# Windowed attention on one core: where the softmax's reciprocal sums are applied, and by which engine

## The chip, the cores and the metric

One core of a Trainium2 chip runs one program. Its engines are named here as in the profile: TensorE (PE, with its weight loads as PEld), VectorE (DVE), ScalarE (ACT), GpSimd (POOL) and SyncE (SP). The metric is the device time of the whole program in microseconds (us). All data is float32 unless a row says otherwise.

## The reference, cut to what matters

The program is a chain of layers over x of 8 x 256 x 128. Two of them are six-layer transformers with windowed attention, and the change lies in these alone. One such layer, for each of the 8 batch rows of 256 positions, with 16 heads of 64:

```
q, k, v = split(x_shifted @ Wqkv)                # 128 -> 3 * 1024
q, k = rotary(l2norm(q)), rotary(l2norm(k))
# windows of 32: a query sees its own window and the one before, causal
sim  = einsum('bhwie,bhwje->bhwij', bq, bk2) * 8
attn = softmax(where(mask, -big, sim))
out  = einsum('bhwij,bhwje->bhwie', attn, bv2)
x    = x + out @ Wo
x    = x + feed_forward(shift(x))                # 128 -> 2 * 341 -> 128, gelu
```

Softmax divides each row of exponentials by its sum. The division may come before the product with V (on the probabilities) or after it (on the context).

## The kernel before, in words

A transformer runs as 48 **turns** (6 layers x 8 batch rows), and there are two transformers, so 96 turns. A turn T has 8 **slots** p; slot p belongs to one **pair** of heads. Each engine has one queue, written out by hand in `pe_window`, `act_window`, `dve_window` and in the loop for GpSimd, and each executes its queue in order; semaphores tie the queues together. Work of several turns is interleaved: in the slots of turn T the engines do the attention of T, the projections ("chunks") and rotations of T + 1, the output product of T - 1 and the feed-forward of T - 2 and T - 3.

The attention of one pair p goes through these steps, with the line of the profile in brackets:

- `pe_scores` (L1716) writes the scores of both heads into banks 0 and 1; VectorE's `dve_negmax` (L2090) adds the mask, writes the result into `c.pairs` and reduces it to a row's extreme; ScalarE's `act_probs` (L1983) takes the exponential in place in `c.pairs`, in four instructions, and gives the row sums.
- `dve_recip` (L2099) takes the reciprocal of the four sums of each partition. `pool_spread` (L1944) copies each reciprocal 64 times into `c.spread` (128 x 256).
- `pe_turn_probs` (L1728, L1729) transposes the unnormalised probabilities into bank 2 in four transposes, at the head of slot p. `act_copy_probs` (L1990) copies them out to `c.pairsT`; `dve_turn_prev` (L2110) transposes the small corner of the window before.
- `pe_shares` (L1738) transposes `c.spread` in two transposes into the upper half of bank 4 or 5, one slot later. `pe_weigh` (L1750) multiplies V with the turned probabilities into the lower half of that bank. ScalarE's `act_copy_shares` (L1995) copies the upper half out, and VectorE's `dve_share` (L2104) multiplies the lower half by it, which gives `ctxT`.

Of the other work, these steps stand in the same queues. TensorE's chunk products (L1784) of turn T + 1, two in each of slots 0 to 5, use banks 6 and 7 in turn. A q or k chunk is squared and copied by ScalarE (L2003, L2007: `act_copy_chunk`, in the next slot of its queue), summed and rotated by VectorE (L2121, L2129: `dve_rotate`), and only then is its bank free for the chunk after the next. A v chunk is copied by ScalarE alone (L2010). GpSimd's `pool_prepare` multiplies by the cosines (L1960), adds (L1967) and scales the keys (L1973): three instructions in slots 1 and 4, four in slots 2 and 5, two in slots 3 and 6, none in 0 and 7. The turned queries are copied by ScalarE (`act_copy_q`, L2015) and the turned keys by VectorE (`dve_copy_k`, L2115). VectorE's `dve_roots` (L2145 to L2151) is a chain of twelve small dependent instructions, in slots 2 and 6; in slot 2 the feed-forward's statistics (L2161 to L2166) stand before it. The output product of T - 1 (L1819) and half of the feed-forward (L1850) are TensorE's in slot 6.

The order inside slot p before: TensorE turns p, turns the shares of p - 1, makes the scores of p + 2, weighs p - 1, then the other work, then two chunks. ScalarE copies the chunks of slot p - 1, copies the turned p, takes the exponentials of p + 1 and copies the shares of p - 1. VectorE takes the reciprocal of p, applies the shares to p - 2, turns the corner of p, rotates, and reduces the scores of p + 2.

Of the kernel before, what the change touches and what calls it, by code (L numbers as in the profile page):

```python
# [16 lines left out]
P = 128  # L17
# [76 lines left out]
def allocate(nc, ctx):  # L94
# [37 lines left out]
    c.shares = sb("shares", [P, 2, S])  # L132
    c.recip = sb("recip", [P, 2, 32])
    c.spread = sb("spread", [P, 2, S])
# [1492 lines left out]
def windowed_transformers(nc, sem, c, name, io):  # L1627
# [7 lines left out]
             "probs_ready", "probsT_in_psum", "probsT_ready", "prev_ready", "recip_ready", "spread_ready", "ctx_in_psum", "shares_ready", "ctx_ready",  # L1635
# [8 lines left out]
     s.probs_ready, s.probsT_in_psum, s.probsT_ready, s.prev_ready, s.recip_ready, s.spread_ready, s.ctx_in_psum, s.shares_ready, s.ctx_ready,  # L1644
# [51 lines left out]
    def run(number):  # L1696
# [24 lines left out]
        def pe_turn_probs(pe, T, p):  # L1721
            pe.wait_ge(s.probs_ready, T * PAIRS + p + 1)
            if T * PAIRS + p > T0 * PAIRS:

                pe.wait_ge(s.probsT_ready, T * PAIRS + p)
            for side in range(2):
                probs, out = c.pairs[:, 2 * (p % 4) + side, :], c.bank[2][:, S * side:S * side + S]
                pe.transpose(out[:, 0:P], probs[:, 0:P], c.ident[:, :])  # L1728
                last = pe.transpose(out[:, P:2 * P], probs[:, P + WINDOW:2 * P + WINDOW], c.ident[:, :])  # L1729
            last.then_inc(s.probsT_in_psum, 1)  # L1730

        def pe_shares(pe, T, p):
            pe.wait_ge(s.spread_ready, T * PAIRS + p + 1)
            if T * PAIRS + p - 1 > T0 * PAIRS:

                pe.wait_ge(s.ctx_ready, T * PAIRS + p - 1)
            for t in range(HALVES):
                pe.transpose(c.bank[4 + p % 2][:, S + t * P:S + (t + 1) * P], c.spread[:, p % 2, t * P:(t + 1) * P],  # L1738
                             c.ident[:, :])

        def pe_weigh(pe, T, p):
            pe.wait_ge(s.probsT_ready, T * PAIRS + p + 1)
            pe.wait_ge(s.prev_ready, T * PAIRS + p + 1)
            if p == 0:
                pe.wait_ge(s.chunk_copied, (T + 1) * N_CHUNKS)
            out = c.bank[4 + p % 2]
            for kt, q0, q1 in ((0, 0, P + WINDOW), (1, P, S)):
                at = 0 if kt == 0 else P + WINDOW
                for side in range(2):
                    last = pe.matmul(out[DH * side:DH * side + DH, q0:q1], V[T % 2][:, kt, 2 * p + side, :],  # L1750
                                     c.pairsT[:, 2 * (p % 2) + side, at:at + q1 - q0], start=(kt == 0), stop=(kt == 1),
                                     skip_group_check=True)
            last.then_inc(s.ctx_in_psum, 1)
# [133 lines left out]
        def pe_window(pe, T):  # L1887
            following = has_turn(T + 1)
            for p in range(PAIRS):
                pe_turn_probs(pe, T, p)  # L1890
                if p >= 1:
                    pe_shares(pe, T, p - 1)
                elif has_turn(T - 1):
                    pe_shares(pe, T - 1, PAIRS - 1)
# [24 lines left out]
                if p == 5 and has_turn(T - 2):  # L1919
                    pe_turn_normed(pe, T - 2)  # L1920

        def pe_tail(pe):
            L = T1 - 1
            pe_shares(pe, L, PAIRS - 1)
# [115 lines left out]
        def act_window(a, T):  # L2040
            following = has_turn(T + 1)
            for p in range(PAIRS):
                if following:
                    for i in ACT_CHUNK_SLOTS.get(p, ()):
                        act_copy_chunk(a, T + 1, i)
                    if p == 6:
                        act_copy_q(a, T + 1, 0)
                act_copy_probs(a, T, p)
# [13 lines left out]
                if p >= 1:  # L2062
                    act_copy_shares(a, T, p - 1)
                elif has_turn(T - 1):
                    act_copy_shares(a, T - 1, PAIRS - 1)
# [6 lines left out]
        def act_tail(a):  # L2072
            L = T1 - 1
            act_copy_shares(a, L, PAIRS - 1)
# [27 lines left out]
        def dve_share(v, T, p):  # L2102
            v.wait_ge(s.shares_ready, T * PAIRS + p + 1)
            v.tensor_tensor(ctxT[T % 2][:, p, :], c.bank[4 + p % 2][:, 0:S], c.shares[:, p % 2, :],  # L2104
                            ALU.mult).then_inc(s.ctx_ready, 1)

        def dve_turn_prev(v, T, p):

            v.wait_ge(s.probs_ready, T * PAIRS + p + 1)
# [98 lines left out]
        def dve_window(v, T):  # L2208
            following = has_turn(T + 1)
            for p in range(PAIRS):  # L2210
# [44 lines left out]
        def dve_tail(v):  # L2255
            L = T1 - 1
            dve_share(v, L, PAIRS - 2)
            dve_share(v, L, PAIRS - 1)
# [9 lines left out]
        with nc.Block() as block:  # L2268
# [50 lines left out]
            def _(g):  # L2319
                for slot in range(PAIRS):  # L2320
                    pool_prepare(g, T0, slot)
                for T in range(T0, T1):
                    for p in range(PAIRS):
                        pool_spread(g, T, p)
# [200 lines left out]
```

## Time and profile before

| | |
|---|---|
| median of 3 runs | 6064.55 us (6064.37 to 6069.54) |
| span of the profiled execution | 6062.1 us |
| the two transformers, from the first turned pair | 683.4 to about 2817 us and 3052 to about 5186 us |
| a turn in the steady state | 44.6 us |
| PE, PEld busy, whole span | 5372.5 us (89%), 3794.5 us (63%) |
| DVE, ACT, POOL busy, whole span | 4241.2 us (70%), 3913.4 us (65%), 2700.1 us (45%) |

The profiled execution is 2.5 us shorter in its span than the median of the runs; the page gives no other time for it. Times in rows count from the start of the span. PE's matmuls are pipelined and the end of one is modelled: the distance between two starts is what TensorE spends on one.

### The profile page before, as it was taken

What the parts mean: (1) busy time and instruction counts of PE and PEld (TensorE: products, weight loads), DVE (VectorE), ACT (ScalarE), POOL (GpSimd) and SP (SyncE); (2) the same over time, 40 slices, a digit from 0 to 9 for tenths busy, and PEclk for the clock granted to TensorE, in tenths of its full rate; (3) what the DMA queues carried; (4) which work ended last, traced back from release to release, by engine and by line L of the source; (5) the groups of instructions that cost most, each with busy time, mean ns of one, the idle gap of its engine ahead of it and who ended that gap; (6) DMA issues with size and microseconds to landing.
All of it is one profiled execution on the core that took longest, in us unless ns stands there. A gap on an engine that the chain in (4) does not pass through costs nothing. (4 is left out here: it accounts for less than half of the span.)

```text
span 6062.1 us, 121575 instructions
## 1 busy us (share of the span) xinstructions
PE 5372.5 (89%) x41154; PEld 3794.5 (63%) x41154; DVE 4241.2 (70%) x16112; ACT 3913.4 (65%) x11510; POOL 2700.1 (45%) x2578
## 2 busy tenths in 40 slices
PE   7885699999999999997489999999999999697989
PEld 5674366666666666665256666666666666464678
DVE  4453688888888888885378888788888887454522
ACT  2211588888888888884178888888888888222333
POOL 0000556556565565652166656566565665230000
PEclk9996799999999999998599999999999999697999
DMA  0000000000000000000000000000000000000000
GB/s 11 22 1 3 22 1 12 9 12 9 1 15 6 12 9 12 8 1 4 21 1 7 10 6 12 9 12 9 4 13 6 12 8 1 5 2 4 2 29 8
DMA packets 30964, 53.45 MB, mean 9 GB/s; under 512 B 7688, under 2 KB 17168, under 8 KB 29712
## 3 DMA queue, kind: packets, MB, share of 16 engines
q1 hardware_dynamic: 30352, 45.66, 2.4%
q8 instruction: 339, 5.55, 0.4%
q14 instruction: 273, 2.24, 0.1%
HBM read 44.60 MB, written 1.05 MB: 8 GB/s over the span
## 5 line engine op out<-in xcount | busy, mean ns | idle before, releaser
L1784 PE MATMUL bank<-wA,next_rowT 128*128 128x512 f32 x2304 | 1213.7, 629 | 194.6 <-DVE turnB L2129 73.1
L1983 ACT ACTIVATE pairs<-pairs,negmax 128x128 f32<-128x128 f32 (+1 forms) x3072 | 1236.8, 418 | 18.6 <-DVE negmax L2090 17.5
L1960 POOL TENSOR_TENSOR turnA<-raw,ropes 128x512 f32<-128x512 f32 x768 | 968.7, 1271 | 169.3 <-ACT raw L2007 140.4
L2090 DVE CUSTOM_DVE_ANT_0 pairs<-bank,bands,big 128x128 f32<-128x128 f32 (+1 forms) x3072 | 941.7, 364 | 64.6 <-PE bank L1716 61.0
L1967 POOL TENSOR_TENSOR qk<-turnA,turnB 128x512 f32<-128x512 f32 x768 | 975.8, 1271 | 0.0
L1944 POOL COPY spread<-recip 128x256 f32<-128x256 f32 x768 | 305.3, 398 | 1257.8 <-DVE recip L2099 1251.4
L1784 PEld LDWEIGHTS bank<-wA,next_rowT 128*128 128x128 f32 x2304 | 369.6, 190 | 676.7 <-DVE turnB L2129 294.3
L1990 ACT ACTIVATE pairsT<-bank 128x512 f32<-128x512 f32 x768 | 465.9, 607 | 302.2 <-PE bank L1729 301.9
L1983 ACT ACTIVATION_READ_ACCUMULATOR pairs<-pairs,negmax 128x1 f32 x3072 | 625.0, 203 | 0.0
L285 POOL TENSOR_TENSOR rstd<-vareps,neg_half 128x2 f32<-128x2 f32 x56 | 39.0, 696 | 1292.4 <-DVE vareps L256 892.7
L2129 DVE TENSOR_TENSOR turnB<-bank,ropes 128x512 f32<-128x512 f32 x768 | 523.1, 681 | 0.0
L1973 POOL TENSOR_TENSOR qk<-qk,big 128x1024 f32<-128x1024 f32 x192 | 365.7, 1905 | 341.3 <-DVE recip L2204 327.9
L1807 PE MATMUL bank<-ident,qk 128*128 128x128 f32 x3072 | 431.1, 279 | 41.5 <-ACT big L2010 16.4
L2007 ACT ACTIVATE raw<-bank 128x512 f32<-128x512 f32 x768 | 461.1, 600 | 0.0
L1807 PEld LDWEIGHTS bank<-ident,qk 128*128 128x128 f32 x3072 | 344.7, 142 | 156.1 <-issue 131.6
L1728 PE MATMUL bank<-ident,pairs 128*128 128x128 f32 x1536 | 383.4, 277 | 27.7 <-ACT pairs L1983 27.7
L1729 PE MATMUL bank<-ident,pairs 128*128 128x128 f32 x1536 | 377.7, 273 | 0.0
L1819 PEld LDWEIGHTS bank<-wB,ctxT 128*128 128x128 f32 x3072 | 357.8, 192 | 8.4 <-issue 0.3
L1819 PE MATMUL bank<-wB,ctxT 128*128 128x128 f32 x3072 | 358.8, 275 | 0.0
L1728 PEld LDWEIGHTS bank<-ident,pairs 128*128 128x128 f32 x1536 | 216.1, 141 | 178.3 <-ACT pairs L1983 90.8
L2104 DVE TENSOR_TENSOR ctxT<-bank,shares 128x256 f32<-128x256 f32 x768 | 306.1, 399 | 8.6
L1850 PE MATMUL bank<-xT,wC 128*128 128x256 f32 (+1 forms) x1152 | 305.4, 402 | 6.9 <-ACT big L2038 3.7
(306 smaller groups left out, 11272.8 us busy)
## 6 DMA issues: line engine op xcount, KB each, us to landing
wA<-in_wt_wqkv SPq DMA_DIRECT2D x72, 256.0 KB, 2.8
wB<-in_wt_wo SPq DMA_DIRECT2D x12, 512.0 KB, 3.5
wC<-in_wt_w SPq DMA_DIRECT2D x12, 341.0 KB, 2.9
wD<-in_wt_w SPq DMA_DIRECT2D x12, 192.0 KB, 2.4
big<-in_e_up SPq DMA_DIRECT2D x1, 2048.0 KB
big<-in_e_down SPq DMA_DIRECT2D x1, 2048.0 KB
scl<-in_wt_scales SPq DMA_DIRECT2D x12, 128.0 KB, 3.1
X<-in_x SPq DMA_DIRECT2D x8, 128.0 KB, 2.5
```

The source lines that it names most:

```text
L1728: pe.transpose(out[:, 0:P], probs[:, 0:P], c.ident[:, :])
L1729: last = pe.transpose(out[:, P:2 * P], probs[:, P + WINDOW:2 * P + WINDOW], c.ident[:, :])
L1784: pe.matmul(side_bank(i)[:, :], c.next_rowT[:, t * P:(t + 1) * P], wqkv[:, k * 512:(k + 1) * 512], start=True, stop=True).then_inc(s.chunk ...
L1807: done = pe.transpose(side_bank(i)[:, (2 * k + t) * P:(2 * k + t + 1) * P], c.qk[:, t, which, at:at + P], c.ident[:, :])
L1819: done = pe.matmul(c.bank[6][:, t * D:(t + 1) * D], ctxT[T % 2][:, k, t * P:(t + 1) * P], wo[:, k * D:(k + 1) * D], start=(k == 0), stop=( ...
L1960: g.tensor_tensor(c.turnA[:, m % 2, :].rearrange("p (h d) -> p h d", h=8), c.raw[:, m % 4, :].rearrange("p (h d) -> p h d", h=8), cos, ALU ...
L1967: g.tensor_tensor(c.qk[:, t, k // 2, (k % 2) * 512:(k % 2) * 512 + 512], c.turnA[:, m % 2, :], c.turnB[:, m % 4, :], ALU.add).then_inc(s.s ...
L1983: last = a.activation(tile, tile, ACT.Exp, scale=-1.0, bias=c.negmax[:, 2 * p + side, t:t + 1], accum_out=c.pair_sums[:, p % 4, t, side:si ...
L1990: a.activation(whole_blocks(c.pairsT[:, 2 * (p % 2):2 * (p % 2) + 2, :]), c.bank[2][:, :].rearrange("p (n k) -> p n k", n=4), ACT.Identity ...
L2007: last = a.activation(c.raw[:, m % 4, :], src, ACT.Identity)
L2090: last = v.tensor_tensor_reduce(c.pairs[:, 2 * (p % 4) + side, AT[t]:AT[t] + SPAN[t]], c.bank[side][:, AT[t]:AT[t] + SPAN[t]], c.bands[:, ...
L2129: v.tensor_tensor(out, turned, sin.unsqueeze(1).broadcast_to((P, 8, 2, DH // 2)), ALU.mult).then_inc(s.chunk_rotated, 1)
```

## The change

GpSimd no longer spreads the reciprocals. It multiplies the probabilities of pair p in place by them (`pool_share_out`: two products, of 2 x 128 and 2 x 160 columns in 128 partitions, the reciprocal repeated along the columns). The transposes of the shares, their copy and VectorE's product are gone; ScalarE copies the finished context from the bank to `ctxT` (`act_copy_ctx`). TensorE's turning of pair p and VectorE's turning of the corner wait for GpSimd (`shared_out`) in place of ScalarE; TensorE turns pair p at the end of slot p, VectorE turns the corner behind the scores' reduction, and ScalarE copies the turned pair p - 1 at the head of slot p, ahead of the chunks (in slot 6 behind the chunks and ahead of `act_copy_q`). The buffers `c.shares` and `c.spread` go.

```diff
         def pe_turn_probs(pe, T, p):
-            pe.wait_ge(s.probs_ready, T * PAIRS + p + 1)
+            pe.wait_ge(s.shared_out, T * PAIRS + p + 1)
...
-        def pe_shares(pe, T, p):
-            pe.wait_ge(s.spread_ready, T * PAIRS + p + 1)
...
         def pe_weigh(pe, T, p):
             pe.wait_ge(s.probsT_ready, T * PAIRS + p + 1)
             pe.wait_ge(s.prev_ready, T * PAIRS + p + 1)
+            if T * PAIRS + p - 1 > T0 * PAIRS:
+
+                pe.wait_ge(s.ctx_ready, T * PAIRS + p - 1)
...
         def pe_window(pe, T):
             following = has_turn(T + 1)
             for p in range(PAIRS):
-                pe_turn_probs(pe, T, p)
-                if p >= 1:
-                    pe_shares(pe, T, p - 1)
-                elif has_turn(T - 1):
-                    pe_shares(pe, T - 1, PAIRS - 1)
                 if p + 2 < PAIRS:
                     pe_scores(pe, T, p + 2)
...
                 if p == 5 and has_turn(T - 2):
                     pe_turn_normed(pe, T - 2)
+                pe_turn_probs(pe, T, p)
...
-        def pool_spread(g, T, p):
+        def pool_share_out(g, T, p):
             g.wait_ge(s.recip_ready, T * PAIRS + p + 1)
-            if T * PAIRS + p - 2 >= T0 * PAIRS:
-
-                g.wait_ge(s.ctx_in_psum, T * PAIRS + p - 1)
-            g.tensor_copy(c.spread[:, p % 2, :].rearrange("p (n d) -> p n d", n=4),
-                          c.recip[:, 0, 4 * (p % 4):4 * (p % 4) + 4].unsqueeze(2).broadcast_to((P, 4, DH))
-                          ).then_inc(s.spread_ready, 1)
+            first = 2 * (p % 4)
+            for t in range(HALVES):
+                tiles = c.pairs[:, first:first + 2, AT[t]:AT[t] + SPAN[t]]
+                recips = c.recip[:, 0, 4 * (p % 4) + 2 * t:4 * (p % 4) + 2 * t + 2]
+                last = g.tensor_tensor(tiles, tiles, recips.unsqueeze(2).broadcast_to((P, 2, SPAN[t])), ALU.mult)
+            last.then_inc(s.shared_out, 1)
...
-        def act_copy_shares(a, T, p):
+        def act_copy_ctx(a, T, p):
             a.wait_ge(s.ctx_in_psum, T * PAIRS + p + 1)
-            a.activation(c.shares[:, p % 2, :], c.bank[4 + p % 2][:, S:2 * S], ACT.Identity).then_inc(s.shares_ready, 1)
+            a.activation(ctxT[T % 2][:, p, :], c.bank[4 + p % 2][:, 0:S], ACT.Identity).then_inc(s.ctx_ready, 1)
...
         def act_window(a, T):
             following = has_turn(T + 1)
             for p in range(PAIRS):
+                if p == 0 and has_turn(T - 1):
+                    act_copy_probs(a, T - 1, PAIRS - 1)
+                elif p not in (0, 6):
+                    act_copy_probs(a, T, p - 1)
                 if following:
                     for i in ACT_CHUNK_SLOTS.get(p, ()):
                         act_copy_chunk(a, T + 1, i)
+                if p == 6:
+                    act_copy_probs(a, T, p - 1)
+                if following:
                     if p == 6:
                         act_copy_q(a, T + 1, 0)
-                act_copy_probs(a, T, p)
...
         def dve_turn_prev(v, T, p):
 
-            v.wait_ge(s.probs_ready, T * PAIRS + p + 1)
+            v.wait_ge(s.shared_out, T * PAIRS + p + 1)
+            if T * PAIRS + p - 1 > T0 * PAIRS:
+                v.wait_ge(s.ctx_in_psum, T * PAIRS + p - 1)
...
                 dve_recip(v, T, p)
-                if p >= 2:
-                    dve_share(v, T, p - 2)
-                elif has_turn(T - 1):
-                    dve_share(v, T - 1, p + PAIRS - 2)
-                dve_turn_prev(v, T, p)
...
                 if p == 0:
                     dve_copy_k(v, T, COPY_LATE_QKT_SLOTS[p])
+                dve_turn_prev(v, T, p)
```

## Rows read from the trace of the kernel before

**Rows 1.** Windows, one steady turn, then its slots (1 and 2 together); start:end, length, busy (instructions), PEclk.
```profile
1477.94:1522.57 44.63, 42.30 (x303) 29.43 (x303) 36.53 (x147) 36.86 (x115) 26.71 (x26) 1.00 0.05 16
1478.50:1484.18 5.68, 5.34 (x38) 3.44 (x36) 3.99 (x17) 4.58 (x16) 0.80 (x2) 1.00 0.12 44
1484.18:1494.45 10.27, 10.27 (x76) 7.23 (x74) 10.12 (x33) 8.98 (x29) 9.13 (x8) 1.00 0.12 34
1494.45:1500.35 5.90, 5.26 (x36) 3.16 (x34) 5.36 (x28) 4.61 (x15) 2.76 (x3) 1.00 0.00 1
1500.35:1504.68 4.33, 4.25 (x28) 2.31 (x26) 4.30 (x15) 4.33 (x15) 4.33 (x5) 1.00 0.00 0
1504.68:1511.29 6.61, 5.56 (x38) 3.38 (x36) 5.07 (x19) 4.69 (x16) 5.76 (x6) 1.00 0.01 2
1511.29:1518.77 7.48, 7.48 (x64) 6.65 (x62) 4.56 (x27) 5.34 (x16) 3.53 (x3) 1.00 0.00 0
1518.77:1523.13 4.36, 4.15 (x36) 3.25 (x34) 3.12 (x14) 4.33 (x13) 0.40 (x1) 1.00 0.01 4
```

**Rows 2.** Timeline of PE, slots 3 to 6: start, length, line, idle before and releaser.
```profile
1498.73 1.12 PE L1784 MATMUL bank<-wA,next_rowT 128*128 128x512 f32 x2 [0.39 <-DVE kT L2115]
1499.70 0.27 PE L1728 MATMUL bank<-ident,pairs 128*128 128x128 f32 x1
...
1504.02 0.27 PE L1728 MATMUL bank<-ident,pairs 128*128 128x128 f32 x1
...
1504.46 0.38 PE L1738 MATMUL bank<-ident,spread 128*128 128x128 f32 x2
1504.77 0.77 PE L1716 MATMUL bank<-kT,qT 64*128 64x128 f32 x8
1505.46 0.71 PE L1750 MATMUL bank<-pairsT,V 128*64 128x160 f32 x8
1506.83 2.32 PE L1784 MATMUL bank<-wA,next_rowT 128*128 128x512 f32 x4 [0.65 <-DVE turnB L2129]
...
1518.44 0.27 PE L1729 MATMUL bank<-ident,pairs 128*128 128x128 f32 x1
```

**Rows 3.** Timeline of ACT, the same stretch.
```profile
1499.90 0.60 ACT L2003 ACTIVATE sq<-bank 128x512 f32<-128x512 f32 x1 [0.43 <-PE bank L1784]
1500.39 0.59 ACT L2007 ACTIVATE raw<-bank 128x512 f32<-128x512 f32 x1
...
1509.67 0.59 ACT L2015 ACTIVATE big<-bank 128x512 f32<-128x512 f32 x1
1518.75 0.60 ACT L1990 ACTIVATE pairsT<-bank 128x512 f32<-128x512 f32 x1 [2.11 <-PE bank L1729]
```

**Rows 4.** Timelines of DVE and POOL, slots 2 to 4.
```profile
1493.19 1.25 DVE L2166 TENSOR_SCALAR big<-big 128x2 f32<-128x2 f32 x1
...
1497.20 0.17 DVE L2099 RECIPROCAL recip<-pair_sums 128x4 f32<-128x4 f32 x1
...
1497.30 0.39 DVE L2104 TENSOR_TENSOR ctxT<-bank,shares 128x256 f32<-128x256 f32 x1
...
1497.99 0.69 DVE L2115 COPY kT<-bank 128x512 f32<-128x512 f32 x1
...
1500.53 0.69 DVE L2121 TENSOR_REDUCE big<-sq 128x8 f32<-128x512 f32 x1
...
1502.32 0.68 DVE L2129 TENSOR_TENSOR turnB<-bank,ropes 128x512 f32<-128x512 f32 x1
...
1493.14 1.27 POOL L1967 TENSOR_TENSOR qk<-turnA,turnB 128x512 f32<-128x512 f32 x1
```

**Rows 5.** Groups by line and form, POOL: busy us, mean ns | idle before, releaser.
```profile
L1973 POOL TENSOR_TENSOR qk<-qk,big 128x1024 f32<-128x1024 f32 x192 | 365.7, 1905 | 341.3 <-DVE recip L2204 327.9
L1944 POOL COPY spread<-recip 128x256 f32<-128x256 f32 x768 | 305.3, 398 | 1257.8 <-DVE recip L2099 1251.4
...
L225 POOL CAST iota<-small 128x16 f32<-128x16 int32 x1 | 0.2, 196 | 0.1
```

**Rows 6.** The instructions of line L2166: ns min/median/max.
```profile
L2166 DVE TENSOR_SCALAR big<-big x96: 170/1246/1259, 779.2 to 5193.1; 128x2 f32<-128x2 f32 x96
```

More of the change, by code:

```diff
@@ L131, in allocate @@
     c.pair_sums = sb("pair_sums", [P, 4, HALVES, 2])
-    c.shares = sb("shares", [P, 2, S])
     c.recip = sb("recip", [P, 2, 32])
-    c.spread = sb("spread", [P, 2, S])
     c.ctx = sb("ctx", [P, HALVES, D])
@@ L1634, in windowed_transformers @@
              "qT_in_psum", "kT_in_psum", "qT_copied", "kT_copied", "scores_ready", "scores_seen", "negmax_ready",
-             "probs_ready", "probsT_in_psum", "probsT_ready", "prev_ready", "recip_ready", "spread_ready", "ctx_in_psum", "shares_ready", "ctx_ready",
+             "probs_ready", "probsT_in_psum", "probsT_ready", "prev_ready", "recip_ready", "shared_out", "ctx_in_psum", "ctx_ready",
              "out_in_psum", "shifted_in_psum", "normed", "normedT_in_psum", "normedT_ready",
@@ L1643, in windowed_transformers @@
      s.qT_in_psum, s.kT_in_psum, s.qT_copied, s.kT_copied, s.scores_ready, s.scores_seen, s.negmax_ready,
-     s.probs_ready, s.probsT_in_psum, s.probsT_ready, s.prev_ready, s.recip_ready, s.spread_ready, s.ctx_in_psum, s.shares_ready, s.ctx_ready,
+     s.probs_ready, s.probsT_in_psum, s.probsT_ready, s.prev_ready, s.recip_ready, s.shared_out, s.ctx_in_psum, s.ctx_ready,
      s.out_in_psum, s.shifted_in_psum, s.normed, s.normedT_in_psum, s.normedT_ready,
@@ L1730, in pe_turn_probs @@
             last.then_inc(s.probsT_in_psum, 1)
-        def pe_shares(pe, T, p):
-            pe.wait_ge(s.spread_ready, T * PAIRS + p + 1)
[L1734 to L1739, printed above, removed]
         def pe_weigh(pe, T, p):
@@ L1920, in pe_window @@
                     pe_turn_normed(pe, T - 2)
+                pe_turn_probs(pe, T, p)
         def pe_tail(pe):
             L = T1 - 1
-            pe_shares(pe, L, PAIRS - 1)
             pe_weigh(pe, L, PAIRS - 1)
@@ L2062, in act_window @@
                 if p >= 1:
-                    act_copy_shares(a, T, p - 1)
+                    act_copy_ctx(a, T, p - 1)
                 elif has_turn(T - 1):
-                    act_copy_shares(a, T - 1, PAIRS - 1)
+                    act_copy_ctx(a, T - 1, PAIRS - 1)
                 if has_turn(T - 2):
@@ L2073, in act_tail @@
             L = T1 - 1
-            act_copy_shares(a, L, PAIRS - 1)
+            act_copy_probs(a, L, PAIRS - 1)
+            act_copy_ctx(a, L, PAIRS - 1)
             for f in (L - 1, L):
@@ L2100, in dve_recip @@
                          c.pair_sums[:, p % 4, :, :].rearrange("p t h -> p (t h)")).then_inc(s.recip_ready, 1)
[L2102 to L2105, printed above, removed]
         def dve_turn_prev(v, T, p):
-            v.wait_ge(s.probs_ready, T * PAIRS + p + 1)
+            v.wait_ge(s.shared_out, T * PAIRS + p + 1)
+            if T * PAIRS + p - 1 > T0 * PAIRS:
+                v.wait_ge(s.ctx_in_psum, T * PAIRS + p - 1)
             v.transpose(c.pairsT[P - WINDOW:P, 2 * (p % 2):2 * (p % 2) + 2, P:P + WINDOW],
@@ L2256, in dve_tail @@
             L = T1 - 1
-            dve_share(v, L, PAIRS - 2)
-            dve_share(v, L, PAIRS - 1)
             dve_ff_add(v, L - 2)
@@ L2323, in _ @@
                     for p in range(PAIRS):
-                        pool_spread(g, T, p)
+                        pool_share_out(g, T, p)
                         if has_turn(T + 1):
```

## The prediction

> **What bounds the kernel now.** I read the windows of one steady turn first, then the timelines of the engines inside its slots, then the groups of GpSimd. The windows [rows 1] show that a turn takes 44.63 us and that TensorE is busy in 42.30 of them, at a granted clock of 1.00, its upper level of 2.4 GHz. ScalarE and VectorE have about 8 us of slack each, GpSimd 18 us. But "TensorE is the bound" holds only by slots. In slots 1, 2 and 6 it is busy throughout. In slots 3 and 5 it is idle for 0.64 and 1.05 us, and its timeline [rows 2] says on what: in slot 5 the chunk waits 0.65 us for a rotation by VectorE, in slot 3 it waits 0.39 us for VectorE's copy of the keys. So there are two rates: TensorE's own instructions, and the circle that frees banks 6 and 7, chunk, ScalarE's square and copy, VectorE's sum and rotation, next chunk but one. The change shortens the first and touches the second.
>
> **The transposes that go.** Four transposes of a pair start 0.44 us apart from the next step (1504.02 to 1504.46 [rows 2]), 0.11 us each. The two of the shares cost 0.22 us; the rest of the 0.31 us up to the scores is the change from one operation to the other and stays. That is 1.77 us of TensorE per turn of 8 pairs, and it is the gain on offer. VectorE loses its product of 0.39 us per pair [rows 4], ScalarE's copy keeps its size and only changes its source and target: nothing is gained there, because in the slots where VectorE is late it is late on something else (below).
>
> **What GpSimd takes on.** The product is not in the trace. The nearest row is the scaling of the keys, also in place with a repeated factor: 1.905 us for 1024 columns [rows 5]. With the 0.196 us of a 16-column instruction as its fixed part it is 1.7 ns a column, so 256 and 320 columns cost 0.60 and 0.71, together 1.3 us. From above: the plain sum, 1.27 us for 512 columns [rows 4], with the same fixed part gives 2.17 ns a column and 1.6 us together. From below: the one-input copy, 0.398 us for 256 columns [rows 5], gives 0.9 us for 576. I take 1.3, the nearest kind. The copy it replaces was 0.4, so GpSimd's load grows from 26.7 to about 34 us a turn. The Trainium skill ("GPSIMD Engine Reference", section 3.1) counts about 2.6 cycles an element for two inputs at 1.2 GHz, which makes an estimate of 1.25 us for the 576 columns before any dispatch, and the sum would not move by it.
>
> **The order that moves.** I follow one slot with P for the moment at which TensorE has issued the last transpose of pair p - 1. The last transpose ends 0.27 after its start, that is at P + 0.16, and ScalarE starts copying 0.04 later (1518.44 + 0.27, then 1518.75 [rows 2, 3]), at P + 0.20. Before, ScalarE copied the chunks of the slot as soon as they were there and the turned pair after them; now the pair comes first, and the pair is turned after the chunks. So the chunks' square cannot start before P + 0.69 (ScalarE's starts lie 0.49 apart [rows 3]) and ends at P + 1.29. VectorE's sum starts 0.03 later (1499.90 + 0.60, then 1500.53 [rows 3, 4]), the second rotation starts 1.79 after that and takes 0.68 [rows 4], so it ends at P + 3.79. The chunk that needed the bank starts 0.05 later (as after the copy of the keys, 1497.99 + 0.69, then 1498.73 [rows 2, 4]), takes 0.97 (1498.73 to 1499.70 [rows 2]), and the turning of pair p, 0.44, follows it. That closes a circle of 5.25 us in every slot with two rotations, 1, 2, 4 and 5, whatever TensorE has to do.
>
> By slots, before [rows 1] and after:
> Slot 0: 5.68, less 0.22, is about 5.5. Here xT stands between the scores and the weighing and hides the copy.
> Slots 1 and 2: 10.27 before, two circles of 5.25 after, 10.5. The saved 0.44 is lost.
> Slot 4: 4.33 before; the circle makes it 5.25.
> Slot 5: its first chunk starts 2.15 into the slot now (1506.83 [rows 2]) and 4.46 are left. In the circle the first rotation comes half a sum-and-rotation pair, about 1.2, before the second, so the chunk starts at P + 2.65; 4.46 less 0.22 follow: 6.9 for 6.61.
> Slot 6: the scores of the next turn's first pair need the turned queries that `act_copy_q` copies. Before, this copy lay at 1509.67, right behind the last chunk and 1.6 us ahead of the slot. Now `act_copy_probs` of pair 5 is in front of it in ScalarE's queue, and waits for TensorE's end of slot 5. So the copy runs from P + 0.69 to P + 1.28, and the scores start at P + 1.33 in place of P + 0.09: 1.24 us in which TensorE waits. 7.48 less 0.22 plus 1.24 is 8.5.
> Slot 7: 4.36 before, with 0.21 idle in front of the first turning [rows 1], which waited for the exponentials; that wait goes with the turning's move. The weighing waits for the copy that ends at P + 0.80 where its own turn is P + 0.78, 0.07 with the step between engines. 4.0.
> Slot 3 is the one with a long chain. In slot 2 GpSimd's four instructions can start when ScalarE's copy of the chunk is there, P2 + 1.8; the product on pair 2 is done by then (slot 1's three instructions of 1.27 from P1 + 1.8 end at P1 + 5.6, 1.3 more is P2 + 1.65). Four of 1.27 end at P2 + 6.9. VectorE's small instruction on the statistics ends only when the fourth does: it took 1.25 us where the shortest of its kind took 0.17 [rows 4, 6], and ended together with the GpSimd instruction that ran. The roots and the rest take 2.79 from there to the reciprocal of pair 3 (1494.41 to 1497.20 [rows 4]), the copy of the keys starts 0.10 behind it, since the shares and the corner no longer lie between, and takes 0.69, then 0.05 to the chunk: P2 + 10.5. With the chunk and the turning the slot ends at P2 + 11.9, and less slot 2's 5.25 that is 6.65 for 5.90. GpSimd's product on pair 3, from P2 + 9.9 to 11.2, is just hidden by that chunk, which TensorE leaves at P2 + 11.5; at 1.6 us in place of 1.3 the product on pair 2 would end at P2 + 1.95, behind ScalarE's copy, and the slot would grow by some 0.2.
>
> The sum is 5.5 + 10.5 + 6.65 + 5.25 + 6.9 + 8.5 + 4.0 = 47.3 us for 44.63: 2.67 us more per turn. The corner's new wait costs VectorE nothing on this path: behind it stand the roots in slot 6, whose delay ends in the wait for TensorE's output product. There are 96 turns; for the start and the tail of the two transformers I count 94. That is 251 us on the profiled span of 6062.1, which lies 2.5 under the median: 6316, and I say **6315 us**.
>
> **Rivals.**
> First, on the other side: the circle has slack that I do not see, ScalarE has its copy in time, and the transposes' 1.77 us come back whole, 94 x 1.77 = 166 us, 5898 us; with the queries' wait of slot 6 left in, 6015. The 42.30 of 44.63 us speak for it. Against it: slot 4 was 4.33 us long and can keep that only if the second rotation ends 0.9 us before P + 3.79, and nothing in the order lets the square start earlier. Chance 0.08. Gains and losses that cancel to within 0.2%: 0.03.
> Second, half a loss: one of the terms in slots 3, 4 or 6 is covered by slack carried from the slot before, and 1.3 us a turn remain, 6190 us. Chance 0.14.
> Third, GpSimd holds VectorE up for longer. In slot 2 one more GpSimd instruction of 1.27 us lies under the roots, because the product is slower or its place in the queue is later. Each of the twelve dependent steps can wait behind one, and the reciprocal, the keys, the chunk and the product on pair 3 all move with it: 94 x 1.27 = 119 us more, 6435 us. For it: the row of 1.25 against 0.17 us [rows 4, 6], which shows that such a wait exists. Against it: GpSimd has nothing to do behind its fourth instruction until the reciprocal of pair 3 is there. Chance 0.15. The Trainium skill ("SBUF — State Buffer", section "Who interferes with whom") has the rule: the two engines share a pair of ports, and one in use by an instruction of either blocks the other's for the whole of it, two-input products on GpSimd included. By that rule every added product is a further chance for such a block; the trace agrees on the block itself, with 1.25 for 0.17 us.
> My forecast has 0.60.
>
> **Range and chances.** 6150 to 6450 us holds the forecast with GpSimd's product between 0.9 and 1.6 us, and the second and third rival; it leaves out the first. Faster by over 0.2% (12 us, about what a measurement of this kernel can tell from no change): 0.08; within: 0.03; slower: 0.89.
>
> **What would show it.** Right: a turn of about 47 us; TensorE idle ahead of the scores in slot 6 with ScalarE's query copy as releaser, 1.2 us each; slot 4 at 5.25 us with chunks that wait for rotations; ScalarE idle ahead of most copies of turned pairs, with TensorE as releaser; GpSimd's two products at 0.6 and 0.7 us. Wrong: rotations that end earlier than 3.8 us into slot 4; products of over 0.9 us each, which would make GpSimd's queue the bound; or turnings that wait for `shared_out`, of which I expect none.

## The result, and the profile after

The changed kernel takes 6386.12 us (median of 4 runs, 6383.85 to 6387.52), the kernel before, timed beside it, 6066.42 us (6064.37 to 6069.54): a ratio of 1.0533 with a 95% interval of 1.0518 to 1.0548. It is slower by 320 us, where 251 were forecast; sign and range held. The span of the profiled execution is 6383.5 us.

First the busy times on the page of the kernel after.

```profile
PE 5286.0 (83%) x39618; PEld 3610.8 (57%) x39618; DVE 4010.3 (63%) x15344; ACT 3877.5 (61%) x11510; POOL 3382.0 (53%) x3346
```

TensorE and VectorE do less than before, as the change says; GpSimd does 682 us more, 7.1 a turn, and is still idle for nearly half of the span. No engine became the bound. Next the windows of one steady turn after, the whole turn and then its eight slots (slots 1 and 2 in one line), with the columns of [rows 1].

```profile
1642.07:1689.92 47.85, 41.38 (x286) 27.46 (x286) 34.03 (x139) 36.45 (x115) 33.80 (x34) 1.00 0.00 1
1642.07:1647.53 5.46, 5.03 (x34) 3.22 (x34) 2.91 (x14) 3.78 (x15) 1.79 (x3) 1.00 0.00 0
1647.53:1658.02 10.49, 10.42 (x72) 6.68 (x70) 8.23 (x29) 8.79 (x28) 9.05 (x10) 1.00 0.01 2
1658.02:1664.76 6.74, 5.11 (x34) 2.94 (x32) 6.16 (x30) 3.91 (x13) 3.71 (x5) 1.00 0.00 0
1664.76:1670.01 5.25, 4.09 (x26) 2.09 (x24) 4.04 (x15) 4.39 (x14) 5.11 (x6) 1.00 0.00 0
1670.01:1676.91 6.90, 5.49 (x36) 3.08 (x34) 5.15 (x17) 5.41 (x16) 6.76 (x7) 1.00 0.01 2
1676.91:1685.40 8.49, 7.32 (x62) 6.41 (x60) 4.44 (x25) 5.86 (x16) 5.73 (x6) 1.00 0.00 1
1685.40:1689.92 4.52, 3.92 (x34) 3.04 (x32) 3.11 (x14) 4.30 (x13) 1.66 (x3) 1.00 0.00 0
```

The turn is 3.22 us longer than in [rows 1], although TensorE is busy for 0.92 us less: its idle time went from 2.33 to 6.47. Seven of the slots' lengths (slots 1 and 2 as a sum) stand within 0.1 us of the forecast; slot 7 does not. What TensorE waits for is in its groups of waits after (total us, number of waits, the longest).

```profile
PE bank L1776 <- DVE turnB L2120: 230.6, 207, 4.8
PE bank L1714 <- ACT big L2002: 87.8, 94, 1.2
PE bank L1714 <- ACT qT L2002: 84.3, 90, 1.2
PE bank L1776 <- DVE kT L2106: 52.6, 48, 1.1
PE bank L1776 <- DVE big L2106: 50.6, 46, 1.1
```

Three things, each once or more in a turn: a chunk (L1776) waits for a rotation of VectorE (L2120) or for VectorE's copy of the keys (L2106), and the scores (L1714) wait for ScalarE's copy of the queries (L2002). A fourth is chunks that wait for that copy, 80 us in 184 short waits, where the kernel before had 56. Their places in the turn are in TensorE's timeline after (start, length, line; idle time ahead and its releaser in brackets).

```profile
1655.43 2.32 PE L1776 MATMUL bank<-wA,next_rowT 128*128 128x512 f32 x4
...
1663.36 1.12 PE L1776 MATMUL bank<-wA,next_rowT 128*128 128x512 f32 x2 [1.12 <-DVE kT L2106]
...
1667.42 2.32 PE L1776 MATMUL bank<-wA,next_rowT 128*128 128x512 f32 x4 [1.10 <-DVE turnB L2120]
...
1678.22 0.77 PE L1714 MATMUL bank<-big 64*128 64x128 f32 x8 [1.18 <-ACT big L2002]
...
1690.01 0.77 PE L1714 MATMUL bank<-big 64*128 64x128 f32 x8 [0.68 <-ACT big L2002]
```

The first row is from slot 2, where no idle time is recorded: its four chunk matmuls take 2.32 us, against 1.94 in the run below without division and with the gate, so the wait of slot 2 stands inside the row.

And ScalarE's timeline after, at the heads of slots 4, 6 and 7:

```profile
1664.96 0.60 ACT L1977 ACTIVATE pairsT<-bank 128x512 f32<-128x512 f32 x1 [2.83 <-PE bank L1727]
1665.45 0.59 ACT L1990 ACTIVATE sq<-bank 128x512 f32<-128x512 f32 x1
...
1677.08 0.60 ACT L1977 ACTIVATE pairsT<-bank 128x512 f32<-128x512 f32 x1 [1.47 <-PE bank L1727]
1677.57 0.59 ACT L2002 ACTIVATE big<-bank 128x512 f32<-128x512 f32 x1
...
1685.59 0.60 ACT L1977 ACTIVATE pairsT<-bank 128x512 f32<-128x512 f32 x1 [2.62 <-PE bank L1727]
1686.21 1.28 ACT L1970 ACT_TABLE_LOAD   x1
...
1689.11 0.36 ACT L1982 ACTIVATE ctxT<-bank 128x256 f32<-128x256 f32 x1
1689.38 0.58 ACT L2002 ACTIVATE big<-bank 128x512 f32<-128x512 f32 x1
```

In slot 4 ScalarE is idle for 2.83 us, until TensorE has turned the pair; the square (L1990) of a chunk that lay ready stands behind that copy. In slot 6 the queries' copy (L2002) is behind it too. In slot 7 a second copy of queries comes last of all, behind the turned pair, the table load, the exponentials and the context, and the scores at 1690.01 wait for it: this one I had not seen.

Last, the first two turns of a transformer, in the windows after; neither has feed-forward work yet, and the first has no output product either,

```profile
685.04:732.23 47.19, 34.98 (x210) 20.38 (x210) 31.40 (x127) 31.67 (x106) 33.74 (x34) 0.93 0.00 1
732.23:780.40 48.17, 39.52 (x250) 24.48 (x250) 31.79 (x128) 32.27 (x108) 33.77 (x34) 0.93 0.00 1
```

and in those of the kernel before:

```profile
684.48:723.59 39.11, 34.09 (x226) 21.49 (x226) 32.88 (x134) 32.42 (x107) 26.64 (x26) 0.97 0.00 1
723.59:764.79 41.20, 38.89 (x268) 25.61 (x266) 33.77 (x136) 31.77 (x107) 26.62 (x26) 0.96 0.01 2
```

Before, such a turn was short because TensorE had little to do; after, it is as long as any other. Turns 0 to 2 took 39.11, 41.20 and 44.13 us and now take 47.19, 48.17 and 47.85. In eight places of TensorE's timeline after, GpSimd itself is the last to come, in the first two turns and the last of each transformer, 16.7 us in all; this is one of the two longest:

```profile
731.28 0.33 PE L1726 MATMUL bank<-ident,pairs 128*128 128x128 f32 x1 [4.03 <-POOL pairs L1932]
```

### The profile page after: what moved, and what is told of

Same layout as the page of the kernel before. It is cut to its first block and busy times, and to the rows that moved or that the text cites. A ratio compares the mean times of both kernels' runs of the same rounds, so it can differ in the third digit from the quotient of the medians.

```text
span 6383.5 us, 117833 instructions
## 1 busy us (share of the span) xinstructions
PE 5286.0 (83%) x39618; PEld 3610.8 (57%) x39618; DVE 4010.3 (63%) x15344; ACT 3877.5 (61%) x11510; POOL 3382.0 (53%) x3346
## 5 line engine op out<-in xcount | busy, mean ns | idle before, releaser
L1776 PE MATMUL bank<-wA,next_rowT 128*128 128x512 f32 x2304 | 1261.3, 641 | 443.5 <-DVE turnB L2120 230.6
L1932 POOL TENSOR_TENSOR pairs<-pairs,recip 128x256 f32<-128x256 f32 (+1 forms) x1536 | 992.8, 668 | 975.2 <-DVE recip L2093 974.2
L1970 ACT ACTIVATE pairs<-pairs,negmax 128x128 f32<-128x128 f32 (+1 forms) x3072 | 1242.8, 424 | 16.7 <-DVE negmax L2084 15.6
L1776 PEld LDWEIGHTS bank<-wA,next_rowT 128*128 128x128 f32 x2304 | 355.7, 190 | 982.7 <-DVE turnB L2120 592.5
L1970 ACT ACTIVATION_READ_ACCUMULATOR pairs<-pairs,negmax 128x1 f32 x3072 | 643.3, 209 | 0.0
L2120 DVE TENSOR_TENSOR turnB<-bank,ropes 128x512 f32<-128x512 f32 x768 | 522.7, 681 | 0.5 <-issue 0.5
L2112 DVE TENSOR_REDUCE big<-sq 128x8 f32<-128x512 f32 x384 | 261.5, 681 | 300.1 <-ACT sq L1990 300.0
L1726 PE MATMUL bank<-ident,pairs 128*128 128x128 f32 x1536 | 379.2, 274 | 16.7 <-POOL pairs L1932 16.7
L1714 PE MATMUL bank<-kT,qT 64*128 64x128 f32 (+1 forms) x3072 | 298.1, 313 | 91.4 <-ACT qT L2002 84.3
L1714 PE MATMUL bank<-big 64*128 64x128 f32 (+1 forms) x3072 | 297.0, 312 | 91.7 <-ACT big L2002 87.8
```

The source lines that it names most:

```text
L1714: last = pe.matmul(c.bank[side][:, AT[t]:AT[t] + SPAN[t]], q[:, t * P:(t + 1) * P], k[:, FIRST_KEY[t]:FIRST_KEY[t] + SPAN[t]], start=True, ...
L1776: pe.matmul(side_bank(i)[:, :], c.next_rowT[:, t * P:(t + 1) * P], wqkv[:, k * 512:(k + 1) * 512], start=True, stop=True).then_inc(s.chunk ...
L1932: last = g.tensor_tensor(tiles, tiles, recips.unsqueeze(2).broadcast_to((P, 2, SPAN[t])), ALU.mult)
L1970: last = a.activation(tile, tile, ACT.Exp, scale=-1.0, bias=c.negmax[:, 2 * p + side, t:t + 1], accum_out=c.pair_sums[:, p % 4, t, side:si ...
L2120: v.tensor_tensor(out, turned, sin.unsqueeze(1).broadcast_to((P, 8, 2, DH // 2)), ALU.mult).then_inc(s.chunk_rotated, 1)
```

## The experiments

The theory: the time is lost to order, because a copy that waits for TensorE's last work of a slot stands ahead of the copies that free TensorE's banks in ScalarE's queue. The rivals: GpSimd's products are the cost, by their own length or by holding VectorE up; or the division's gain was never there. A slot is counted here from one start of the scores to the next, so the wait ahead of the scores of slot 6 counts to slot 5; by this cut the medians of the kernel after are 5.46, 5.25, 5.25, 6.74, 5.25, 8.12, 7.27 and 4.52 us for slots 0 to 7.

**GpSimd's products taken out.** The division is left out: TensorE's turning and VectorE's corner wait for the exponentials, and the products are not made.

```diff
-            pe.wait_ge(s.shared_out, T * PAIRS + p + 1)
+            pe.wait_ge(s.probs_ready, T * PAIRS + p + 1)
...
-            v.wait_ge(s.shared_out, T * PAIRS + p + 1)
+            v.wait_ge(s.probs_ready, T * PAIRS + p + 1)
...
-                        pool_share_out(g, T, p)
```

> The changed kernel without GpSimd's products: the turnings wait for the exponentials, as before, in the changed order. It leaves the division by the row sums out. Theory (the order costs the time, GpSimd's products are hidden): 6355 to 6386 us, slots 1, 2 and 4 still 5.25 us long. Rival (GpSimd's load or the ports it blocks cost the time): at most 6066 us, since TensorE keeps the saving of 1.77 us a turn.

Measured: 6547.11 us, ratio 1.0805 (1.0787 to 1.0823). With 1.3 us of work less per slot it is slower than the kernel after. All slots are as after but slot 3, whose median went from 6.74 to 8.11. The timelines of VectorE and GpSimd in this run say why:

```profile
1791.37 0.98 DVE L2157 TENSOR_SCALAR big<-big 128x2 f32<-128x2 f32 x1
1792.38 1.21 DVE L2136 TENSOR_SCALAR big<-big 128x34 f32<-128x34 f32 x1
1793.62 0.18 DVE L2137 TENSOR_SCALAR ints<-big 128x34 int32<-128x34 int32 x1
...
1791.04 2.50 POOL L1954 TENSOR_TENSOR qk<-turnA,turnB 128x512 f32<-128x512 f32 x2
```

Two additions of GpSimd now run without a gap under VectorE's roots, and two small instructions are caught, the second for 1.21 us in place of 0.18. That makes slot 3 7.76 us long where the granted clock stays at 1.00; in about half of the turns the clock falls behind the longer idle time as well, as in this window of slot 3:

```profile
1690.72:1699.85 9.13, 6.47 (x34) 3.54 (x32) 7.35 (x30) 3.90 (x13) 4.88 (x4) 0.83 0.00 0
```

The product had also been a gate: it waits for the reciprocal of pair 3, which VectorE makes behind the roots, and the addition stands behind it in GpSimd's queue. The next run puts the gate back without the work.

```diff
-                        pool_share_out(g, T, p)
+                        g.wait_ge(s.recip_ready, T * PAIRS + p + 1)
```

> The changed kernel without GpSimd's products, but GpSimd still waits for the reciprocals where each product stood. It leaves the division by the row sums out. In the run without that wait GpSimd's fifth instruction ran under the roots of slot 2 and slot 3 took 8.11 us. Theory (the order costs the time, and the wait alone keeps that instruction off the roots): slot 3 back at 6.7 us, the other slots as in the changed kernel, 6370 to 6390 us. Rival (the products themselves cost time): below 6300 us.

Measured: 6375.48 us, ratio 1.0526 (1.0511 to 1.0542), beside 1.0533 for the kernel after: the intervals overlap. The window of its slot 3:

```profile
1652.09:1658.89 6.80, 5.10 (x34) 2.95 (x32) 6.21 (x30) 3.90 (x13) 3.62 (x4) 1.00 0.01 1
```

So in the steady turns the 1.3 us of GpSimd's products per slot cost nothing: the 44 later turns of the first transformer take 2110.0 us without them and 2106.7 with them. They do cost in the first turns: the first three take 43.90, 45.48 and 47.90 us here, 137.3 together in place of 143.2, about 6 us in each transformer, and the spans differ by 10.6. All but that of the loss is there without the products. Next, every product also made into a spare tile, ahead of the one in place:

```diff
+            for t in range(HALVES):
+                g.tensor_tensor(c.spare[:, t, :, 0:SPAN[t]], c.pairs[:, first:first + 2, AT[t]:AT[t] + SPAN[t]],
+                                c.recip[:, 0, 4 * (p % 4) + 2 * t:4 * (p % 4) + 2 * t + 2].unsqueeze(2)
+                                .broadcast_to((P, 2, SPAN[t])), ALU.mult)
```

> The changed kernel with every product made once more into a spare tile, 1.29 us more of GpSimd per pair. Theory (the product is just hidden in slots 2, 3 and 7, so more of it shows there, about 2.1 us in slot 3, 0.7 in slot 4, 1.9 in slot 7): about 6800 us. Rival (GpSimd is far from the path, 3 us of idle time in every second slot): 6386 to 6450 us. If GpSimd's load alone set the time, 8 x 1.29 x 94 = 970 us more, 7350 us.

Measured: 7003.48 us, ratio 1.1553 (1.1536 to 1.157), some 200 us more than expected. The windows of one of its turns, of slots 3 and 4 in it, and TensorE's timeline there:

```profile
1772.03:1826.50 54.47, 46.01 (x286) 30.14 (x286) 35.67 (x139) 36.53 (x114) 43.72 (x50) 0.91 0.00 1
1789.26:1798.62 9.36, 5.79 (x34) 3.16 (x32) 7.34 (x30) 3.90 (x13) 6.38 (x8) 0.93 0.00 0
1798.62:1804.94 6.32, 6.25 (x25) 3.39 (x24) 4.67 (x16) 4.39 (x14) 6.18 (x8) 0.56 0.00 0
```
```profile
1797.66 0.48 PE L1727 MATMUL bank<-ident,pairs 128*128 128x128 f32 x1 [0.91 <-POOL pairs L1939]
1798.70 1.33 PE L1715 MATMUL bank<-kT,qT 64*128 64x128 f32 x8
```

GpSimd is busy for 43.72 of 54.47 us, so its load is not the bound even then. In slot 3 TensorE idles for 3.57 us, 0.91 of them directly on the product and 2.14 on VectorE's copy of the keys (1.12 in the kernel after), and in slot 4 TensorE works at a granted clock of 0.56, near the lower of its two levels (1.2 GHz): the scores take 1.33 us in place of 0.77. So one product is hidden; two are not, and the stall is paid a second time through the clock.

**ScalarE's order.** First slot 6 alone: the queries' copy ahead of the turned pair's.

```diff
+                if p == 6 and following:
+                    act_copy_q(a, T + 1, 0)
                 if p == 6:
                     act_copy_probs(a, T, p - 1)
-                if following:
-                    if p == 6:
-                        act_copy_q(a, T + 1, 0)
```

> The changed kernel with one swap in ScalarE's queue in slot 6: the copy of the next turn's queries ahead of the copy of turned pair 5. Theory (TensorE's wait ahead of slot 6's scores is this copy, 1.17 us a turn): 94 x 1.1 us less, 6280 us, and that wait gone from the profile. Rival (another wait takes its place, the copy of the turned pair, VectorE's copy of the keys): 6350 to 6386 us.

Measured: 6316.53 us, ratio 1.0419 (1.0404 to 1.0435), 70 us below the kernel after. Slot 5 by this cut fell from 8.12 to 7.12; of the 1.24 us that the prediction gave to the queries' copy 1.0 comes back. Over 94 turns that would be more than 70 us, and 6280 was expected; slot 3 takes 7.5 us or more in 20 of 90 turns of this run, in the kernel after in 2, and that is some 20 us (a run below shows what happens in such a slot). Next the circle: ScalarE's chunk copies first again, and TensorE weighs later, so that it does not wait for the pair's copy instead.

```diff
-                elif p not in (0, 6):
-                    act_copy_probs(a, T, p - 1)
                 if following:
                     for i in ACT_CHUNK_SLOTS.get(p, ()):
                         act_copy_chunk(a, T + 1, i)
-                if p == 6:
+                if p >= 1:
                     act_copy_probs(a, T, p - 1)
...
-                if p >= 1:
+                if p in (6, 7):
                     pe_weigh(pe, T, p - 1)
...
+                if p in (1, 2, 3) or (p in (4, 5) and not following):
+                    pe_weigh(pe, T, p - 1)
                 if following:
-                    pe_prepare(pe, T + 1, p, False)
+                    pe_prepare(pe, T + 1, p, False, (lambda: pe_weigh(pe, T, p - 1)) if p in (4, 5) else None)
```

The last argument is called between the two chunks of the slot.

> The changed kernel with ScalarE's copies of the chunks ahead of its copy of the turned pair again, in slots 1 to 5, and with TensorE's weighing behind its other work of the slot (in slots 4 and 5 between the two chunks), so that it need not wait. Theory (the circle of 5.25 us comes from ScalarE's order): slots 1 and 2 at 5.03 and 4.8 us, slot 4 near 4.3, slot 3 near 5.6, slot 5 with its wait near 7.5; 94 x 2.9 us less than 6386, 6110 us. Rival (the pair's late turning or GpSimd holds the chunks up, not ScalarE's order): slots 1, 2 and 4 stay at 5.25, 6350 to 6386 us.

Measured: 6127.07 us, ratio 1.0113 (1.0098 to 1.0128): 259 of the 320 us are back, with GpSimd's products in place. The windows of its slots 3 and 4:

```profile
1602.04:1607.54 5.50, 4.97 (x34) 2.94 (x32) 5.02 (x25) 4.50 (x15) 2.67 (x4) 1.00 0.00 0
1607.54:1612.03 4.49, 3.95 (x26) 2.09 (x24) 4.24 (x15) 4.19 (x15) 4.35 (x5) 1.00 0.00 0
```

The circle of 5.25 us is gone from slots 2 and 4 (4.95, 4.49); slot 1 takes 5.22, in which TensorE is busy throughout. Slot 3 is shorter than in [rows 1], and it gives the most back, 1.23 us a turn by the medians: GpSimd's last instruction of slot 2, under which VectorE's roots stand, ends 0.7 us into slot 3 in place of 1.75. The turn is 45.09 us; slot 5 by this cut, with the queries' wait, is still 7.68, to 6.61 before. The two orders, ScalarE's and TensorE's, were not changed one without the other.

**The wait that I had not seen.** In slot 7 TensorE turns the next queries and keys right behind the scores, and ScalarE takes the next exponentials ahead of the turned pair's copy, so that the last copy comes sooner.

```diff
+                if p == 7 and following:
+                    for i in PE_QKT_SLOTS[p]:
+                        pe_turn_qk(pe, T + 1, i)
...
                 elif p not in (0, 6):
+                    if p == 7 and following:
+                        for side in range(2):
+                            act_probs(a, T + 1, 0, side)
                     act_copy_probs(a, T, p - 1)
```

> The changed kernel with two moves in slot 7: TensorE turns the next turn's queries and keys right behind the scores, ahead of the weighing, and ScalarE takes the next turn's first exponentials while it would wait for pair 6. Theory (the term that the prediction missed, 0.5 us a turn in slot 7, is the wait of the next turn's scores for the copy of these queries): slot 7 at 3.8 to 4.0 us in place of 4.52, 94 x 0.6 us less, 6330 us. Rival (slot 7 is held by GpSimd's product on pair 7): 6375 to 6390 us.

Measured: 6355.52 us, ratio 1.049 (1.0474 to 1.0505), 31 us below the kernel after. Slot 7 lost its whole wait, 4.52 to 3.86, and over some 88 turns that would be 58 us. The rest went in slot 3. Its windows in two turns of this run that follow each other, with the second one's slot cut into pieces:

```profile
3307.92:3314.65 6.73, 5.11 (x33) 2.94 (x32) 6.14 (x30) 3.90 (x13) 3.69 (x5) 1.00 0.00 0
3355.10:3363.01 7.91, 6.29 (x34) 3.35 (x33) 6.22 (x30) 3.90 (x13) 4.73 (x6) 0.85 0.00 0
...
3357.00:3359.00 2.00, 1.49 (x8) 0.65 (x6) 1.70 (x9) 2.00 (x10) 0.00 (x0) 1.00 0.00 0
3359.00:3361.00 2.00, 0.89 (x2) 0.32 (x2) 1.89 (x11) 0.11 (x1) 1.22 (x2) 0.89 0.00 0
3361.00:3363.01 2.01, 2.01 (x7) 0.88 (x5) 0.84 (x6) 0.00 (x0) 1.87 (x3) 0.50 0.00 0
```

The same 34 matmuls (the record of one is missing in the first row) take TensorE 5.11 and 6.29 us. After its idle time of about 1.6 us in the slot its granted clock goes to 0.50, the lower level, for the chunk and the turning. In 28 of 90 turns of this run slot 3 takes 7.5 us or more, in the kernel after in 2 of 90; 26 more at some 1.15 us are 30 us, which is the rest. Why the clock falls in these turns and not in their neighbours I did not settle.

**VectorE's roots freed of GpSimd.** The addition that runs under the roots moves to slot 3, behind the gate, and the scaling of the keys to slot 4.

```diff
-POOL_SLOTS = {1: ("cos0", "cos1", "add0"), 2: ("cos2", "add1", "cos3", "add2"), 3: ("add3", "scale0"),
-              4: ("cos4", "cos5", "add4"), ...
+POOL_SLOTS = {1: ("cos0", "cos1", "add0"), 2: ("cos2", "add1", "cos3"), 3: ("add2", "add3"),
+              4: ("scale0", "cos4", "cos5", "add4"), ...
```

> The changed kernel with GpSimd's last add of slot 2 moved behind the product on pair 3, and its first scaling of the keys behind the product on pair 4. Theory (VectorE's roots stand still while that add runs): the small instruction on the statistics at 0.17 us in place of 0.96, slot 3 at 6.0 us in place of 6.74, 94 x 0.7 us less, 6320 us. Rival (the roots are long for themselves): no difference, 6375 to 6390 us.

Measured: 6313.85 us, ratio 1.0416 (1.0399 to 1.0433), 72 us below the kernel after, as expected. The small instruction on the statistics over the run, and the window of slot 3:

```profile
L2157 DVE TENSOR_SCALAR big<-big x96: 169/170/171, 799.0 to 5454.8; 128x2 f32<-128x2 f32 x96
```
```profile
1645.55:1651.49 5.94, 5.11 (x34) 2.94 (x32) 5.36 (x30) 3.90 (x13) 2.48 (x4) 1.00 0.00 0
```

Shortest, median and longest are 0.17 us; before they were 0.170, 1.246 and 1.259 [rows 6]. Slot 3 fell by 0.80.

**What the transposes are worth.** The kernel before, without the spreading, the shares' transposes and VectorE's product; ScalarE copies the context.

```diff
-            a.activation(c.shares[:, p % 2, :], c.bank[4 + p % 2][:, S:2 * S], ACT.Identity).then_inc(s.shares_ready, 1)
+            a.activation(ctxT[T % 2][:, p, :], c.bank[4 + p % 2][:, 0:S], ACT.Identity).then_inc(s.ctx_ready, 1)
...
-                        pool_spread(g, T, p)
```

The calls of `pe_shares` and `dve_share` go too.

> The kernel before, in its own order, without the spread, the transposes of the shares and VectorE's product; ScalarE copies the contexts out. It leaves the division by the row sums out, and so shows what was to be gained in that order. If TensorE's saving counts where TensorE has no idle time (slots 0, 1, 2 and 6, 0.22 us each): 94 x 0.88 us less, 5985 us. If VectorE's saved product counts too, in slots 3 to 5 where it is late (0.42 us for each of five pairs): another 2 us a turn, about 5800 us. If neither is on the path: 6066 us.

Measured: 6022.50 us, ratio 0.9938 (0.9923 to 0.9953), 38 us above what was expected of TensorE's saving alone. Slot 3 grew from 5.90 to 6.62 for the reason of the first experiment: the spreading had been the gate, and now two instructions of the roots take 1.16 and 1.20 us. With the gate put where the spreading was, as above:

> The kernel before without spread, share transposes and VectorE's product, as in the run without division, and with GpSimd's wait for the reciprocals kept. It leaves the division by the row sums out. Theory (what the run without division did not gain was GpSimd's add under VectorE's roots in slot 3): slot 3 near 5.4 us in place of 6.62, 94 x 1.2 us less than 6022, 5910 us. Rival (VectorE's or ScalarE's order holds slot 3): 6000 to 6022 us.

Measured: 5930.19 us, ratio 0.9793 (0.9777 to 0.9809), 43.27 us a turn. This is the gain on offer in that order: 1.36 us a turn of the 1.77 that the prediction worked out for TensorE.

**All of it together.** ScalarE's and TensorE's order as in the two runs above, the next exponentials ahead of the turned pair in slot 7, where TensorE weighs behind its half of the feed-forward, and the second scaling of keys moved to GpSimd's slot 7.

> The run with the chunks first, and the queries' copy ahead of the pair in slot 6, the exponentials of the next turn's first pair ahead of the pair in slot 7, GpSimd's second scaling of keys behind the product on pair 7, and TensorE's weighing in slot 7 behind its feed-forward product. Theory: the waits ahead of slot 6 (1.17 us), of the next turn's scores (0.55) and of the product on pair 7 go as well; a turn of 43.0 to 43.5 us, 5930 to 5970 us, faster than both kernels. Rival (GpSimd's queue, 35 us a turn with its waits, then sets the time): a turn of 44.5 us or more, 6060 us or more.

Measured: 6016.39 us, ratio 0.9932 (0.9917 to 0.9947), 46 us above the expected range: slot 3 is still 5.53 us. Then the addition moved behind the roots too, once with the queries of slot 7 turned early,

> The reordered run with both of these: the early turning of queries and keys in slot 7, and GpSimd's add behind the roots. Theory: slot 7 at 3.8 to 4.0 in place of 4.32 us, slot 3 at 4.8 in place of 5.52; a turn of 42.9 us, 94 x 1.1 us less than 6016, about 5915 us. Rival (GpSimd's products on pairs 4 to 7 come later and take it back): 5980 to 6016 us.

measured: 6076.49 us, ratio 1.0028 (1.0017 to 1.0039), a miss. Slots 3 and 7 took 4.71 and 6.17: TensorE's turning of the next queries now waits in slot 7, and behind it everything else, as its timeline in this run shows,

```profile
1615.53 1.06 PE L1801 MATMUL bank<-ident,qk 128*128 128x128 f32 x8 [1.87 <-DVE hT L2172]
```

and once without that:

> The reordered run (6016 us) with GpSimd's add behind the roots alone; TensorE turns the next turn's queries in slot 7 where the changed kernel does, at its end. In the run with both moves slot 7 took 6.17 us, with 1.87 us of TensorE waiting ahead of that turning. Theory (TensorE stood in front of an operation whose condition VectorE fulfils only after its roots, and those wait for GpSimd's product on pair 6; at the slot's end the same wait is mostly hidden): slot 3 at 4.7, slot 4 at 4.3, slot 7 about 4.9; a turn of 43.4 us, 5960 us. Rival (GpSimd's product on pair 6 takes the gain back wherever the turning stands): slot 7 at 5.5 us or more, 6016 us or more.

Measured: 5941.25 us (5939.11 to 5943.36), ratio 0.9802 (0.9785 to 0.9818): faster than both kernels. Its windows, the turn, then slots 3 and 4:

```profile
1549.44:1592.67 43.23, 40.80 (x286) 27.78 (x286) 33.65 (x139) 36.94 (x114) 33.72 (x35) 1.00 0.00 1
1565.18:1569.89 4.71, 4.71 (x34) 3.02 (x32) 4.30 (x24) 4.28 (x15) 2.17 (x3) 1.00 0.00 0
1569.89:1574.16 4.27, 3.95 (x26) 2.09 (x24) 4.21 (x15) 4.27 (x15) 4.27 (x5) 1.00 0.00 0
```

GpSimd carries the same 33.7 us as in the kernel after, and the turn is as long as in the run without division and with the gate. That the two are equal is chance: this run is longer in slots 0, 1, 2, 4 and 7 and shorter by 0.96 us in slot 3. Of the 1.41 us a turn that it gains on the kernel before, 1.2 come in slot 3, where the addition no longer lies under the roots. The kernel before with that addition moved, and its division as it was, was not run, so how much of the gain belongs to the new place of the division is not shown.

## Why the prediction was right, and where it was mis-sized

**The circle** stands as worked out. Slots 1 and 2 took 10.49 us and slot 4 5.25, to the forecast's 10.5 and 5.25; ScalarE idled for 2.83 us ahead of the turned pair's copy in slot 4, with TensorE as releaser. In slot 2 the wait is inside the row of chunk matmuls (2.32 us for 1.94), and slot 1 is only 0.22 us longer than without division (5.03), of which the chunks first gave 0.03 back. That ScalarE's order is the cause is shown by putting the chunks first again, with TensorE's weighing placed to suit: 259 us came back, with GpSimd's products and the late turning in place.

**Slots 3, 5 and 6** took 6.74, 6.90 and 8.49 for 6.65, 6.9 and 8.5, with the releasers that were named. The block of VectorE by GpSimd that lengthens slot 3 stands in the timelines after,

```profile
1658.83 0.97 DVE L2157 TENSOR_SCALAR big<-big 128x2 f32<-128x2 f32 x1
...
1658.49 1.28 POOL L1954 TENSOR_TENSOR qk<-turnA,turnB 128x512 f32<-128x512 f32 x1
```

and is shown by moving that addition (and the scaling of the keys behind it): 72 us. The Trainium skill ("SBUF — State Buffer", section "Who interferes with whom") has the two engines share a pair of ports as an exclusive lock; the trace agrees on the block, with 0.17 us where no GpSimd instruction overlaps and 0.97 in the kernel after.

**GpSimd's products** are 0.614 and 0.721 us, taken from its groups by shape after; 0.60 and 0.71 were worked out from the scaling of the keys. In the steady turns they are hidden, as the run with the gate alone shows.

```profile
L1932 POOL TENSOR_TENSOR pairs<-pairs,recip 128x320 f32<-128x320 f32 x768 | 553.9, 721 | 0.0
L1932 POOL TENSOR_TENSOR pairs<-pairs,recip 128x256 f32<-128x256 f32 x768 | 471.5, 614 | 975.2 <-DVE recip L2093 974.2
```

**Slot 7 is the term that was mis-sized**: 4.0 forecast, 4.52 measured. I followed the weighing's wait for the turned pair's copy in it, and the new first place of that copy through ScalarE's queue in slot 6, but not in slot 7, where the second copy of queries stands last. Advancing it took the wait away.

**The multiplier was the second miss.** I counted 94 turns at 2.67 us. The number of turns is right, twice 47, but they are not alike. In each transformer 44 later turns went from 1964.1 to 2106.7 us, 3.24 each, and the first three from 124.4 to 143.2, 18.8 us in place of 8. The step that failed is taking the steady turn's difference for all. The circle sets a floor, so that slots which were short before lose more: slots 1 and 2 of the first turn went from 3.91 and 4.26 to 5.25 each, with the products or without, and take 4.41 each with the chunks first. About 6 of the 18.8 us are GpSimd's products, by the run with the gate alone, in slots 7 and 0 of these turns. Together, twice 142.6 and 18.8 are 322.8 us, against 321.4 between the spans. Also, "turnings that wait for `shared_out`, of which I expect none" was wrong for these turns, with one of 4.03 us and 16.7 in all.

**The rivals.** That the circle has slack fell with slot 4. Half a loss fell too: no term was covered. One more GpSimd instruction under the roots did not come in the kernel after, but it is what the run without products shows, at 1.02 us in slot 3 and what the clock adds; the product's wait for the reciprocal kept it out. I had named that wait as the argument against, and had not seen that GpSimd's copy had served as the same gate in the kernel before.

## What to carry to other kernels

Where work is moved to the end of a stage, look at what its consumer stands in front of in another engine's queue: here 1.3 us of new work per slot was free in the steady turns, and the place of a 0.6 us copy, with the weighing that waits for it, cost 259 us. Before taking a semaphore wait or a small operation away, ask what it held back by accident, since work that starts earlier can land on a chain that it slows down. A loss that comes from a fixed circle is a floor on a stage and not a sum to add, so that the stages that were shortest lose most.

## What the runs showed of the hardware that was not expected

GpSimd with less to do made the kernel slower: without its products 6547 us, with only their wait 6375, because VectorE's instruction of 0.18 us takes 1.21 when a 1.27 us addition of GpSimd overlaps it. A dependent chain can be caught twice, 0.98 and then 1.21.

TensorE's granted clock falls in single slots behind idle time: to 0.50 at the end of slot 3 of the turn shown, and in 28 of 90 turns of that run the slot is longer by some 1.15 us, and to 0.56 over slot 4 with the products made twice. A stall in one slot is then paid again in the matmuls behind it.

The clock went down there behind two gaps of TensorE of 0.51 and 1.11 us, with matmuls between them, and the turn before it had the same two gaps at a clock of 1.00.

A GpSimd product with a repeated operand took 0.614 us for 256 columns and 0.721 for 320, so 1.67 ns a column and about 0.19 us beside that.
